# Perceiver block on one core, delta-rule stage: the place of ScalarE's normalisation of the next rows among its copies at the seam between two periods

## The reference, cut to what matters

```python
x = hidden_states                       # 128 sequences of 32 tokens, 512 wide
h = _rms(x, attn_norm_w)
q = silu(silu(_causal_dwconv(h @ Wq.T, conv_q)))
k = silu(silu(_causal_dwconv(h @ Wk.T, conv_k)))
v = silu(silu(_causal_dwconv(h @ Wv.T, conv_v)))
q = _l2norm(q); k = _l2norm(k)          # 32 heads of 16
beta = jax.nn.sigmoid(h @ Wbeta.T)
def step(S, inp):                       # over the 32 tokens
    kt, qt, vt, bt = inp
    err = jnp.einsum('bhvk,bhk->bhv', S, kt) - vt
    S = S - bt[..., None, None] * err[..., None] * kt[..., None, :]
    o = jnp.einsum('bhvk,bhk->bhv', S, qt)
    return (S, o)
x = x + _rms(o, out_norm_w) @ Wout.T
```

## Time and profile before

| What | us |
|---|---|
| Runs: median of 3 (lowest to highest) | 3098.22 (3088.08 to 3102.05) |
| The profiled execution, its own time | 3096.83 |
| Span of its trace, first to last instruction | 3095.0 |
| Mean granted TensorE clock, share of full speed | 0.932 |
| TensorE matmuls busy | 2768.4 (89%) |
| VectorE busy | 1992.2 (64%) |
| ScalarE busy | 1440.4 (47%) |
| GpSimd busy | 1009.1 (33%) |

### The profile page before, as it was taken

The page is one execution under the profiler, slowest core; times in us unless marked ns, Lnnn a source line. Parts: engine busy times, 40 slices in busy tenths (PEclk is TensorE's granted clock), DMA queues, the critical chain, the costliest instruction groups (busy, mean ns, idle before and its releaser), DMA issues. The chain is left out here.

```text
span 3095.0 us, 66716 instructions
## 1 busy us (share of the span) xinstructions
PE 2768.4 (89%) x26968; PEld 1471.6 (48%) x26968; DVE 1992.2 (64%) x2991; ACT 1440.4 (47%) x2378; POOL 1009.1 (33%) x713
## 2 busy tenths in 40 slices
PE   6999999686988988988747999999999799999997
PEld 2444444252554544544424444444444366666664
DVE  3444444459999899899992444444552377777776
ACT  2222222375867867768613322222222256666664
POOL 0000000107537438356380000000000177777776
PEclk9999999888988988989867999999999899999999
DMA  6999888500000000000211112322210111111110
GB/s 238 337 335 333 309 278 309 182 15 1 2 29 2 29 29 2 29 13 19 102 68 43 68 55 82 123 82 96 99 38 28 66 36 39 39 40 40 41 44 31
DMA packets 126284, 290.20 MB, mean 94 GB/s; under 512 B 30480, under 2 KB 35216, under 8 KB 121968
## 3 DMA queue, kind: packets, MB, share of 16 engines
q1 hardware_dynamic: 122608, 261.85, 24.2%
q10 hardware_dynamic: 3456, 25.17, 2.4%
HBM read 244.96 MB, written 42.01 MB: 93 GB/s over the span
## 5 line engine op out<-in xcount | busy, mean ns | idle before, releaser
L2121 POOL TENSOR_TENSOR d_zb<-d_za 128x1024 f32<-128x1024 f32 x32 | 75.4, 2355 | 986.5 <-DVE d_za L2183 986.5
L899 PE MATMUL b_e<-b_hT,s_region 128*128 128x512 f16 x1152 | 276.0, 385 | 10.3 <-DVE s_region L1325 6.4
L1627 PE MATMUL c_r<-c_hT,c_g_pair 128*128 128x512 f16 x1056 | 255.5, 394 | 13.1 <-DVE c_hT L1790 13.1
L1801 DVE SCALAR_TENSOR_TENSOR c_av<-c_r,c_sg 128x512 f32<-128x512 f32 x88 | 60.8, 691 | 301.5 <-PE c_r L1627 241.3
L1988 PE MATMUL d_m<-s_region,d_xiT 128*128 128x512 bf16 x1024 | 237.7, 383 | 6.5 <-ACT d_sg L2073 2.0
L1627 PE MATMUL c_r<-c_hT,c_u_pair 128*128 128x512 f16 x1056 | 242.9, 380 | 0.0
L1627 PE MATMUL c_d<-c_d_pair,c_aT 128*128 128x512 f16 x1056 | 241.0, 379 | 0.0
L1325 DVE SCALAR_TENSOR_TENSOR s_region<-b_e,b_cw,s_region 128x496 f32<-128x496 f32 (+2 forms) x288 | 203.0, 716 | 18.3 <-ACT s_region L1115 9.9
L851 POOL TENSOR_TENSOR b_tmp<-b_L,s_hn 128x496 f32<-128x496 f32 (+30 forms) x124 | 122.7, 990 | 246.3 <-ACT b_L L1098 236.9
L851 POOL TENSOR_TENSOR b_tmp<-b_L,b_U 128x496 f32<-128x496 f32 (+30 forms) x124 | 130.7, 1054 | 213.0 <-ACT b_L L1098 203.6
L1627 PEld LDWEIGHTS c_r<-c_hT,c_g_pair 128*128 128x128 f16 x1056 | 105.7, 101 | 146.0 <-issue 15.6
(11 more groups left out here) (255 smaller groups left out, 6038.7 us busy)
## 6 DMA issues: line engine op xcount, KB each, us to landing
a_cT<-in_ctxT SPq DMA_DIRECT2D x128, 512.0 KB, 9.8
a_cn<-in_ctx SPq DMA_DIRECT2D x128, 512.0 KB, 9.0
a_x_ln<-in_x SPq DMA_DIRECT2D x8, 1024.0 KB, 15.6
a_cw<-in_ctx SPq DMA_DIRECT2D x128, 64.0 KB, 9.5
a_x_res<-in_x SPq DMA_DIRECT2D x32, 256.0 KB, 10.9
x<-a_x_out SPq DMA_DIRECT2D x32, 256.0 KB, 10.7
b_xg<-x SPq DMA_DIRECT2D x8, 1024.0 KB, 5.5
om<-b_hT SPq DMA_DIRECT2D x32, 256.0 KB, 2.1
```

What stands on the lines that cost most here:

```text
L899: mm = pe.matmul(p[:], w_qkv[:, a, i, n, c * P:(c + 1) * P], hp[:, b, n, :], start=(n + a + b == 0), stop=(n == DC - 1 and a == 1))
L1627: mm = pe.matmul(out, x, y, start=start and i == 0, stop=stop and i == 2)
L1801: V.scalar_tensor_tensor(av[:], p[:], AS / (WS * HS), sg[:, f % 2, :], ALU.mult, ALU.mult)\
L2121: nc.gpsimd.tensor_tensor(o[:, :, 0, :], a[:, :, 0, :], a[:, :, 1, :], ALU.add).then_inc(bf, 1)
```

## The change

In ScalarE's program `rows_normal(g)` goes from behind `right_side(k, 1)` to the very front of the period, and `right_side(k, 2)` from ahead of `rows(g)` to behind it, next to `right_side(k, 3)`. No instruction is added or taken away, and the programs of the other engines stay as they are.

```diff
             for k in range(-1, NG + 1):
                 prev, cur, nxt = k >= 1, 0 <= k < NG, k + 1 < NG
                 g = k + 1
+                if cur and nxt:
+                    rows_normal(g)
                 if cur:
                     right_side(k, 0)
                     right_side(k, 1)
-                if cur and nxt:
-                    rows_normal(g)
-                if cur:
-                    right_side(k, 2)
                 if nxt:
                     rows(g)
                 if k < 0:
...
                 if cur:
+                    right_side(k, 2)
                     right_side(k, 3)
                     for i in range(NL):
                         system(k, i)
```

## The result

The changed kernel takes 3105.28 us (median of 19 runs, 3101.13 to 3111.25) against 3098.13 for the kernel before (19 runs, 3088.08 to 3102.05). The ratio is 1.0026, with a 95% interval of 1.0018 to 1.0034: slower by 7.2 us, and within the 0.5% that was called the same. The forecast was 3103.2 us in a range of 3091 to 3113.

The account below looks back on a forecast made before the run. VectorE was taken to bound the delta stage, TensorE close behind, with ScalarE's seam timeline deciding. Seams' +6.3 and -1.3 made +5.0 on 3096.83, 3101.8; with 1.4 for the median, 3103.2 us, range 3091 to 3113.

Parts of the forecast that it names:

- The load: At seams 3 to 7 ScalarE idles for the load with V0 and V1 queued behind; mean +1.27 us, five seams +6.3.
- the sum: Over the seven seams: +6.3 us at seams 3 to 7 and -1.3 at seams 1 and 2, in all +5.0.
- the estimate: From the skill's DMA rule: the 4 KB load alone would land in 2.0 us, where the trace had 5.4.
- Seams 1 and 2: Load issued long before, so only short waits go: -0.6 us at seam 1, -1.3 for the two.
- The short waits ahead of the high halves: At the seams, V0 and V1 give TensorE more time to turn the rows, so ScalarE's short waits vanish.
- the systems: Behind V2 and V3 at the seam, TensorE turns L2 and L3 late but in time for ScalarE's copies; cost nothing.
- the third rival: At each of seven seams the systems wait for V3's bank: 0.9 us more each, +6.4, 3109.6 us; chance 0.08.
- the fourth: Behind the systems, a new gap keeps TensorE at 1.2 GHz into q0 and k0: +19 us, 3122; chance 0.05.
- The late start reaches the end: At the seam, a microsecond ScalarE gains or loses ahead of its last system copy moves the whole period.
- The second rival: VectorE wins the late start back at TensorE's spreads, up to 4.3 us each: no change, 3098 us; chance 0.13.

Follow-up runs that it names:

- e1: Kernel before with only the normalisations moved to the front, V2 left ahead of the high halves; 3103.6 us against 3092.9, ratio 1.0034.
- e3: Changed kernel's order with the 1 MB load cut into four tiles and the 4 KB load issued first; 3099.5 us against before's 3092.9, ratio 1.0025.
- e4: Kernel before with three extra ScalarE copies ahead of V3's copy at each of seven seams; 3106.9 us against 3092.9, ratio 1.0041.
- e11: Changed kernel with eight unread matmuls filling TensorE's mid-period gap in six periods; 3088.2 us against before's 3096.8, ratio 0.9971.
- e10: Kernel before with eight unread matmuls filling TensorE's mid-period gap in six periods; 3077.9 us against 3096.8, ratio 0.9939.
- e12: Kernel before with V2, V3 ahead of the high halves, load in four behind the 4 KB, unread matmuls in the gap; 3072.1 us against 3092.8, ratio 0.9931.

## Why the prediction was right, and where it was not

**The load (right).** ScalarE waits for it at all five seams from 3 on, 1.42 to 2.89 us, with V0 and V1 behind it, and it landed 5.5 to 6.9 us after its issue (5.4 to 7.1 before). The five seams became 6.1 us longer; the sum said 6.3. e1 shows that moving the normalisations alone gives it (+6.3 at the five seams), and e3 that an earlier landing takes 4.4 of the 6.1 back. In e3, where the 4 KB are issued first, they land 1.9 us after their issue ahead of four of the five late seams (3.4 ahead of the other); behind the 1 MB, at the same seams, no trace has less than 5.4. The 1.9 agrees with the fixed 2.0 us that the Trainium skill (DMA: Bandwidth & Descriptors, Anatomy of one DMA) gives, though the section fits them to DMAs issued from GpSimd and these go out from SyncE. What the estimate left out is the place in the line.

**Seams 1 and 2 (wrong).** The sum had -1.3; they came out +0.36. The short waits ahead of the high halves went, as said. But the step "the systems", costed at nothing, failed there: ScalarE now waits for TensorE ahead of the fifth and sixth copy. The timeline of ScalarE at seam 1 of the changed kernel, and TensorE's with it:

```profile
681.45 2.25 ACT L1098 COPY b_L<-b_r 128x512 f32<-128x512 f32 x4
683.87 0.58 ACT L1098 COPY b_L<-b_r 128x512 f32<-128x512 f32 x1 [0.18 <-PE b_r L869]
684.73 1.56 ACT L1098 COPY b_L<-b_r 128x512 f32<-128x512 f32 x3 [0.27 <-PE b_r L869]
```

```profile
677.53 1.04 PE L869 MATMUL b_r<-s_ident,s_region 128*128 128x128 f32 x8
680.99 4.62 PE L869 MATMUL b_r<-s_ident,s_region 128*128 128x128 f32 x24 [2.42 <-ACT s_hn L1089]
```

TensorE turns L0 and L1, then stands still for 2.42 us until V2 is copied, and has six systems left, at 0.77 each where the earlier trace rows gave 0.56. The standstill alone is not the cause. In e3 TensorE stands still at seam 1 for the same time, and yet no copy of a system waits:

```profile
680.37 0.66 PE L871 MATMUL b_r<-s_ident,s_region 128*128 128x128 f32 x4 [2.41 <-ACT s_hn L1092]
681.24 2.54 PE L871 MATMUL b_r<-s_ident,s_region 128*128 128x128 f32 x20 [0.21 <-ACT s_hn L1092]
```

The granted clock over these transposes differs, 0.63 in the changed kernel and 1.00 in e3:

```profile
681.00:685.60 4.60, 4.60 (x25) 4.17 (x26) 0.13 (x1) 4.15 (x8) 0.00 (x0) 0.63 0.39 126
```

```profile
680.40:685.00 4.60, 4.39 (x31) 3.23 (x32) 0.11 (x1) 4.60 (x9) 0.00 (x0) 1.00 0.33 126
```

At 1.00 TensorE turns a system in 0.51 us, as fast as ScalarE copies one. e1 shows the same at its seams 1 (standstill 2.48, clock 1.00, no wait) and 2 (standstill 2.46, clock 0.80 over all the systems, waits of 0.54). So this is the third rival and the fourth together, in a mild form: the new gap ahead of the systems is followed by the low clock, not in the projections but in the systems themselves. The waits are 0.45 to 0.6 us, not 0.9, at two seams, not seven; seam 1 takes 12.53 in e3 and 13.30 here. Why the clock falls behind the same standstill in one kernel and not in the other stays open.

**The late start reaches the end (right, one for one only roughly).** The second rival, that VectorE wins it back at the spreads, is refuted by e4: 12.8 us more in the seams gave 14.0 by the medians (9 to 17 by the interval) and 10.6 in the stage of the trace. e11 against e10, with bodies 1.1 apart, leaves the seams' 6.6 of a stage that is 7.8 longer.

**The clock (missed).** The fourth rival looked for a low clock in the projections behind the seam. There it was 1.00 in both kernels. Besides seams 1 and 2 the clock matters in mid-period, some 55 to 80 us behind the seam. The bodies grew by 4.5 us. Of these 3.6 are the second body, short in before and long in the changed kernel; the rest is spread over bodies that are long in both. The prediction treated all but the seam as fixed, and that is the step that failed. The rows for it were there: VectorE's 19.6 us of waiting for the spreads had a longest of 4.3, but the 12 waits were not looked at one by one. So the total came near the forecast with some luck. The sum had +5.0; the stage of the trace grew by 11.0, and the span by 8.3 only since the part in front of the stage was 2.8 shorter, which is scatter. In the medians the difference is 7.2, between the seams alone (6.5) and both (11.0). How much of the bodies' 4.5 a typical run pays stays open: they are seen in two traces of each kernel.

## What to carry to other kernels

Before moving a waiting instruction to the front of an in-order engine, compare the time at which the engine comes free with the time at which what it waits for arrives. If the second is later, the ready work behind it was the cover, and moving it costs just that (here +6.1 us at five seams, against 6.3 worked out). Short copies are best spent one group on each wait: here V0 and V1 over the load, V2 and V3 over TensorE's turning of the rows. And when a small shift changes periods elsewhere, look at TensorE's granted clock in each of them; a few matmuls that nobody reads in a gap that is there anyway were worth 19 us, and the best reordering 8.

## What was not expected of the hardware

Eight matmuls of 128x512 in fp16 that nobody reads, put into a gap of about 4 us in six periods, made the kernel 0.6% faster (ratio 0.9939, 0.9926 to 0.9953). In 17 of the 18 bodies of e10 to e12 TensorE's granted clock is 1.00 throughout the first output tile behind them, whose eight fp32 matmuls then take 3.68 us and not the 5.2 to 6.7 of the long bodies. And the place where the clock comes back can repeat from run to run: the changed kernel's six bodies were equal to 0.1 us in two traces, though seam 1 began 2.1 us earlier in one of them. In the two traces of before four of six were. And a standstill of TensorE of 2.4 us was followed at once by a granted clock of 0.63 in the changed kernel and by 1.00 in e3, at the same seam.
